# A two-layer decoder on one core: the third stage's queues written out in another order, with masks, maxima and row sums on eight heads at a time

## The chip, the cores and the metric

The kernel runs on one core of a Trainium2 chip. The metric is the device time of one execution in microseconds (us), and a kernel's figure is the median of several executions. A core has five engines that matter here, each with its own queue that it works off in order: TensorE (PE, with PEld for its weight loads), VectorE (DVE), ScalarE (ACT), GpSimd (POOL) and SyncE (SP), which here only issues DMAs. They meet through semaphores: an instruction can wait until a count is reached, and can raise one when it is done.

## The reference, cut to what matters

There are 16 sequences of 128 rows by 128 features (x), each with a context of 120 rows. Layer 0 is cross-attention and a feed-forward part; layer 1 is another cross-attention, with 16 heads of 64 and a relative position term, and a product in int8:

```python
hq, hk, hv = q @ Wq, k @ Wk, v @ Wv                      # q = layernorm(x); 16 heads of 64
attn = hq.hk + shift(hq.head_r) + hk.ub_w + shift(head_r.vb_w)
attn = where(mask, -INF, attn / sqrt(128)); attn = softmax(attn over the 120 context rows)
out = (attn @ hv) * sigmoid(q @ head_w)                  # a gate for each head
x = x + layernorm(out @ Wo + q) * ln_g + ln_b
x = x + dequantize(int8(layernorm(x)) @ int8(rhs))       # absmax scale of each row
```

All of it is float32 except the int8 product, whose integers travel as bfloat16.

## The kernel before

The work runs in three stages, one after another with some overlap: `attn0` (attention of layer 0), `ffn0` (its feed-forward part) and `layer1` (all of layer 1). In each the unit of work is one sequence t, 0 to 15, and the code is a software pipeline: `layer1(s, par)` is one step of the third stage, written out for every engine by hand, and each piece of it works on the sequence t = s - k for a lag k of its own. `run_steps` calls the steps s = -2 to 23; `on(t)` drops the pieces whose t is outside 0 to 15, so the first and last steps hold little. Steps 10 and 11 are the body of a loop of one round; it has no bearing on the order. What orders the work is thus only the order in which the pieces stand in each engine's `layer1`, and the waits.

A sequence passes through the stage so. DVE and POOL form the layer norm (`rstd`, `xn`), PE transposes it (`xnT`). PE forms queries (`hq_ps`, halves of 8 heads), keys (`hk_ps`) and values (`hv_ps`); ACT and DVE move them out of PSUM as `qv`, `qu`, `kT`, `hv`. PE multiplies `qv` by the position table `rT` (`rel_ps`, four groups of 32 products); ACT copies the results to `relw`; SP stores them to DRAM (`store`) and reads them back shifted (`shifted`, giving `relr`). PE forms the content scores (`content`), DVE adds `relr` to them (`added0` to `added3`, four heads of 120 columns each), applies the mask (`masked`), and takes the negative maxima (`nmax`). ACT exponentiates head by head with the row sum in `ssum`, in pairs of heads (`exp_heads`). DVE turns `ssum` and the gate's `ez` into a factor (`fden`, `rsum`), POOL scales the probabilities with it (`scale_probs`, four heads at a time, L381), PE transposes them (`probT_ps`), ACT copies them (`probT`), PE multiplies by `hv` (`av`), ACT copies (`oT_pairs`), PE applies `wo` (`y_ps`), DVE adds `xn_all` (`u`) and takes statistics (`ovar`). POOL and DVE finish the norm (`rstd_o`, `onorm`, `og`, `x_done`), and then come the norm and the quantization for the int8 part (`xf`, `tiny`, `qx`, `qxi`), its transpose and product (`qT_ps`, `acc_ps`), and the output (`fin`, stored by SP).

The tiles prob, nmax, ssum, rsum, ez, relw, relr, qv, qu, kT, hv are rings of two. PSUM is one tensor PS of eight banks, and `freed(...)` in front of a product waits until the bank's last reader is through; which bank a product writes and whom it waits for is part of the order.

Each of mask, maximum and row-sum factor works on one group of four heads in this kernel, so a step has four masks (DVE L995, L855, L878, L901), four maxima (L858, L861, L937, L945) and four pairs of factor and reciprocal (L843 to L850, L883 to L890).

## Time and profile before

| | us |
|---|---|
| runs of the kernel (three) | 459.0, 452.06, 458.26; median 458.26 |
| the profiled execution | 454.79 |
| its span, first to last instruction | 453.0 |
| PE busy | 415.2 (92% of the span) |
| DVE busy | 398.8 (88%) |
| ACT busy | 375.1 (83%) |
| POOL busy | 264.2 (58%) |

The third stage fills the span from about 165 us on. The profile is of one execution: 1.79 us of its time lie outside the span. Busy time of PE overstates it a little, since matmuls overlap and their ends are modelled; of a wait it is told which instruction ended it.

### The profile page before, as it was taken

Reading aid. Unit: us, or ns where it says so; the run is one execution under the profiler, and the core shown is the slowest. Engines: PE = TensorE matmul, PEld = TensorE weight load, DVE = VectorE, ACT = ScalarE, POOL = GpSimd, SP = SyncE. Lnnn points to the kernel's source line nnn. Section 1 sums busy time; section 2 is a strip of 40 time slices with the busy share of each in tenths; the row PEclk is TensorE's granted clock in tenths of the full one; section 3 lists DMA queues with packets and bytes.
Section 4 is the critical chain, followed back from the end, with each engine's and each line's share of the span. In section 5 each row is a group of like instructions: output and inputs, shape, how many; then the busy total and the mean of one; then the engine's idle time right before and its main releaser. Section 6 shows DMA issues by size and latency. Waiting matters only on the chain.

```text
span 453.0 us, 16761 instructions
## 1 busy us (share of the span) xinstructions
PE 415.2 (92%) x6147; PEld 313.1 (69%) x6147; DVE 398.8 (88%) x1300; ACT 375.1 (83%) x1483; POOL 264.2 (58%) x370
## 2 busy tenths in 40 slices
PE   7999999998789998889999999989999989998871
PEld 6555556555457777778888877868887878887560
DVE  5899999989679985799789999999999999999855
ACT  1999999998845556699989989988998999898941
POOL 4388888878966640044346357447447545646775
PEclk9999999999899999999999999999999999999796
DMA  7250000000000005887447564754754754764000
GB/s 213 58 193 26 14 11 6 11 8 15 2 2 0 0 2 138 216 208 205 120 106 191 156 146 120 190 133 104 198 134 110 198 147 94 186 163 100 8 7 23
DMA packets 54392, 44.88 MB, mean 99 GB/s; under 512 B 43952, under 2 KB 49328, under 8 KB 54320
## 3 DMA queue, kind: packets, MB, share of 16 engines
q1 hardware_dynamic: 53616, 43.59, 37.8%
q8 instruction: 46, 0.75, 0.7%
q10 hardware_dynamic: 704, 0.32, 0.3%
q14 instruction: 26, 0.21, 0.2%
HBM read 22.92 MB, written 20.97 MB: 97 GB/s over the span
## 4 chain that ended last, share of the span: by engine, by line
PE 44%; DVE 44%; issue 4%; ACT 3%; POOL 2%; DMA 1%; SPq 1%; POOLq 0%; DVEq 0%; ACTq 0%
PE PS L1003 37%; DVE prob L855 3%; PE PS L1019 3%; DVE xf L906 2%; DVE prob L901 2%; PE PS L1213 2%; DVE prob L989 1%; DVE nmax L861 1%; PE PS L1179 1%; DVE prob L995 1%; DVE prob L878 1%; DVE prob L865 1%; DVE prob L867 1%; DMA wr<-in_wr 1%; DVE qu L896 1%
## 5 line engine op out<-in xcount | busy, mean ns | idle before, releaser
L381 POOL TENSOR_TENSOR prob<-prob,rsum 128x480 f32<-128x480 f32 x64 | 69.1, 1091 | 85.4 <-DVE rsum L846 80.9
L533 ACT ACTIVATE prob<-prob,nmax 128x120 f32<-128x120 f32 x256 | 102.3, 440 | 1.0 <-DVE nmax L937 1.0
L449 ACT ACTIVATE prob<-PS,nmax 128x120 f32<-128x120 f32 x256 | 89.6, 394 | 4.3 <-DVE nmax L769 2.6
L324 POOL TENSOR_TENSOR prob<-prob,rsum 128x480 f32<-128x480 f32 x64 | 62.5, 988 | 23.2 <-DVE rsum L742 12.8
L533 ACT ACTIVATION_READ_ACCUMULATOR prob<-prob,nmax 128x1 f32 x256 | 63.0, 246 | 0.0
L449 ACT ACTIVATION_READ_ACCUMULATOR prob<-PS,nmax 128x1 f32 x256 | 61.5, 240 | 0.0
L1003 PE MATMUL PS<-rT,qv 64*32 64x152 f32 x2048 | 42.7, 293 | 5.8 <-DVE uo L933 3.8
L1003 PEld LDWEIGHTS PS<-rT,qv 64*32 64x32 f32 x2048 | 30.6, 105 | 21.6 <-issue 18.5
L1003 PEld LDWEIGHTS PS<-xnT,wq 128*128 128x128 f32 x288 | 37.1, 191 | 8.8 <-issue 7.3
L1003 PE MATMUL PS<-xnT,wq 128*128 128x128 f32 x288 | 42.7, 284 | 0.1
L1003 PE MATMUL PS<-ctx,wk 128*128 128x120 f32 x288 | 41.0, 278 | 0.0
L1003 PE MATMUL PS<-wv,ctx 128*120 128x512 f32 (+1 forms) x96 | 40.3, 501 | 0.0
L1003 PE MATMUL PS<-probT,hv 120*64 120x128 f32 x512 | 36.4, 286 | 3.2 <-ACT probT L618 3.2
L1003 PE MATMUL PS<-kT,qu 64*128 64x120 f32 x512 | 35.8, 279 | 3.0 <-ACT relw L632 2.0
L1003 PEld LDWEIGHTS PS<-ctx,wk 128*128 128x128 f32 x288 | 35.9, 191 | 2.2 <-issue 2.2
L1003 PE MATMUL PS<-wo,oT_pairs 128*128 128x128 f32 x256 | 35.9, 284 | 1.0 <-ACT oT_pairs L568 1.0
L1003 PE MATMUL PS<-relw,qT 32*128 32x480 f32 x128 | 34.4, 613 | 0.4 <-DVE relw L747 0.4
L1003 PEld LDWEIGHTS PS<-probT,hv 120*64 120x64 f32 x512 | 28.3, 140 | 8.8 <-ACT probT L618 3.7
L1003 PEld LDWEIGHTS PS<-kT,qu 64*128 64x128 f32 x512 | 31.5, 188 | 4.2 <-ACT relw L632 2.6
L1003 PEld LDWEIGHTS PS<-wo,oT_pairs 128*128 128x128 f32 x256 | 31.9, 196 | 2.5 <-ACT oT_pairs L568 1.8
L1019 PEld LDWEIGHTS PS<-ident,prob 64*120 64x120 f32 x512 | 18.2, 138 | 19.1 <-issue 19.1
L416 POOL TENSOR_TENSOR rstd<-ve,mhalf 128x1 f32<-128x1 f32 x16 | 8.7, 544 | 34.4 <-DVE ve L660 34.4
(195 smaller groups left out, 1128.5 us busy)
## 6 DMA issues: line engine op xcount, KB each, us to landing
rel_scratch<-relw SPq DMA_DIRECT2D x128, 152.0 KB, 3.1
relr<-rel_scratch SPq DMA_DIRECT2D x64, 240.0 KB, 4.2
ctx<-in_ctxT SPq DMA_DIRECT2D x32, 60.0 KB, 1.9
out_x<-fin SPq DMA_DIRECT2D x16, 64.0 KB, 3.2
x_all<-in_x SPq DMA_DIRECT2D x1, 640.0 KB, 7.1
wr<-in_wr SPq DMA_DIRECT2D x1, 512.0 KB, 5.4
wq<-in_wq SPq DMA_DIRECT2D x1, 512.0 KB, 3.6
wk<-in_wk SPq DMA_DIRECT2D x1, 512.0 KB, 4.4
```

The lines of the kernel that those rows point to most:

```text
L324: return pool.tensor_tensor(pr, pr, cols(rsum[p], g, HG).unsqueeze(2).to_broadcast([S, HG, SK]), ALU.mult)
L381: return pool.tensor_tensor(pr, pr, cols(rsum[p], g, HG).unsqueeze(2).to_broadcast([S, HG, SK]), ALU.mult)
L416: pool.tensor_tensor(rstd[p][:, 0:1], ve[p][:, 0:1], mhalf[:, :], ALU.pow).then_inc(A1["rstd"], 1)
L449: last = act.activation(cols(prob[p], n, SK), cols(scores, q, SK), ACT.Exp, bias=nmax[p][:, n:n + 1], accum_out=ssum[p][:, n:n + 1])
L533: last = act.activation(cols(pr, n, SK), cols(pr, n, SK), ACT.Exp, bias=bias[:, n:n + 1], accum_out=total[:, n:n + 1])
L855: dve.scalar_tensor_tensor(out=sc, in0=cap[p][:, :].unsqueeze(1).to_broadcast([S, HG, SK]), scalar=NEG, in1=sc, op0=ALU.add, op1=ALU.min). ...
L861: dve.tensor_reduce(out=cols(nmax[p], 1, HG), in_=heads(cols(prob[p], 1, HG * SK), HG), op=ALU.max, axis=AX.X, negate=True).then_inc(A1["n ...
L901: dve.scalar_tensor_tensor(out=sc, in0=cap[p][:, :].unsqueeze(1).to_broadcast([S, HG, SK]), scalar=NEG, in1=sc, op0=ALU.add, op1=ALU.min). ...
L906: dve.tensor_scalar(xf[p][:, :], row(x_all, t), mv3[p][:, 0:1], rstd3[p][:, :], ALU.subtract, ALU.mult)\
L1003: return pe.matmul(o, a, b, start=start, stop=stop)
L1019: last = pe.transpose(PS[0:SK, bank, q * S // 2:(q + 1) * S // 2], cols(prob[p], g * HG + q, SK)[rows], ident_sb[rows, rows])
L1213: last = pe.transpose(PS[0:SK, bank, q * S // 2:(q + 1) * S // 2], cols(prob[p], g * HG + q, SK)[rows], ident_sb[rows, rows])
```

## The change

Only `layer1` changes, in all five queues, and with it `run_steps`, which calls one step less.

1. The pieces stand in another order on every engine, and in other PSUM banks. Some work on another sequence within a step: the first half of the queries (`hq_ps`, `qv0`, `qu0`) on t = s + 1 in place of s; the last two groups of position products on s - 1 in place of s; one half of the values on s - 1 in place of s - 2; the quantization's first part (`xf` to `inv`) on s - 5 in place of s - 6, its product on s - 6 in place of s - 7. The exponentials of heads 8, 9, 12 and 13, before on s - 2, are now on s - 3 like those of 10, 11, 14 and 15, so all of the second half's stand in one step.
2. The four position groups have a semaphore each (`rel_ps0` to `rel_ps3`).
3. Mask, maximum and factor work on eight heads at a time: two of each in a step, 960 and 8 columns wide, in place of four. The four additions of `relr` stay as they are, four heads each. POOL still scales four heads at a time, but two of the four scalings now wait for nothing but the one before.

The core of the diff:

```diff
-            peeled(layer1, LOOPS[2][1], NB + 8)
+            peeled(layer1, LOOPS[2][1], NB + 7)
...
 @block.gpsimd, layer1:
-                    pool.wait_ge(A1["rsum"], 4 * t + 1)
+                    pool.wait_ge(A1["rsum"], 2 * t + 1)
+                    scale_probs(p, 0).then_inc(A1["scaled0"], 1)
                     scale_probs(p, 1).then_inc(A1["scaled1"], 1)
...
 @block.vector, layer1:
                     dve.wait_ge(A1["probs"], 4 * t + 2)
-                    dve.scalar_tensor_tensor(out=cols(rsum[p], 1, HG), in0=cols(ez[p], 1, HG), scalar=1.0,
-                                             in1=cols(ssum[p], 1, HG), op0=ALU.add, op1=ALU.mult).then_inc(A1["fden"], 1)
-                    dve.wait_ge(A1["fden"], 4 * t + 1)
-                    dve.reciprocal(cols(rsum[p], 1, HG), cols(rsum[p], 1, HG)).then_inc(A1["rsum"], 1)
...
+                    dve.scalar_tensor_tensor(out=cols(rsum[p], 0, 2 * HG), in0=cols(ez[p], 0, 2 * HG), scalar=1.0,
+                                             in1=cols(ssum[p], 0, 2 * HG), op0=ALU.add, op1=ALU.mult).then_inc(A1["fden"], 1)
+                    dve.wait_ge(A1["fden"], 2 * t + 1)
+                    dve.reciprocal(cols(rsum[p], 0, 2 * HG), cols(rsum[p], 0, 2 * HG)).then_inc(A1["rsum"], 1)
...
-                    dve.wait_ge(A1["added1"], t + 1)
-                    sc = heads(cols(prob[p], 1, HG * SK), HG)
+                    dve.wait_ge(A1["added0"], t + 1)
+                    sc = heads(cols(prob[p], 0, 2 * HG * SK), 2 * HG)
...
-                    dve.tensor_reduce(out=cols(nmax[p], 0, HG), in_=heads(cols(prob[p], 0, HG * SK), HG), op=ALU.max, axis=AX.X,
+                    dve.tensor_reduce(out=cols(nmax[p], 0, 2 * HG), in_=heads(cols(prob[p], 0, 2 * HG * SK), 2 * HG), op=ALU.max, axis=AX.X,
```

DVE, at a step of the full pipeline, before: from the mask of the first four heads to that of the last four. prob is the scores' tile, rsum the factor, cap the mask, nmax the maxima.

```order
L995 SCALAR_TENSOR_TENSOR prob<-cap,prob 128x480 [waits a1_added0]
L843 SCALAR_TENSOR_TENSOR rsum<-ez,ssum 128x4 [waits a1_probs]
L846 RECIPROCAL rsum<-rsum 128x4 [waits a1_fden]
L847 SCALAR_TENSOR_TENSOR rsum<-ez,ssum 128x4
L850 RECIPROCAL rsum<-rsum 128x4 [waits a1_fden]
L855 SCALAR_TENSOR_TENSOR prob<-cap,prob 128x480 [waits a1_added1]
L858 TENSOR_REDUCE nmax<-prob 128x4 [waits a1_masked]
L861 TENSOR_REDUCE nmax<-prob 128x4 [waits a1_masked]
L865 TENSOR_TENSOR prob<-PS,relr 128x480 [waits a1_relr11,a1_content]
L867 TENSOR_TENSOR prob<-PS,relr 128x480
L872 TENSOR_SCALAR uo<-uo,mv_o,rstd_o 128x128 [waits a1_orstd]
L878 SCALAR_TENSOR_TENSOR prob<-cap,prob 128x480 [waits a1_added3]
```

The same place now, where a step of DVE begins:

```order
L858 SCALAR_TENSOR_TENSOR rsum<-ez,ssum 128x8 [waits a1_probs]
L861 RECIPROCAL rsum<-rsum 128x8 [waits a1_fden]
L866 SCALAR_TENSOR_TENSOR prob<-cap,prob 128x960 [waits a1_added0]
L869 TENSOR_REDUCE nmax<-prob 128x8 [waits a1_masked]
L874 TENSOR_SCALAR uo<-uo,mv_o,rstd_o 128x128 [waits a1_orstd]
L879 TENSOR_SCALAR qx<-xf,tiny 128x128 [waits f1_inv]
L881 TENSOR_SCALAR xf<-qx 128x128 [waits f1_round]
L883 TENSOR_SCALAR qxi<-xf 128x128 [waits f1_clip]
L887 COPY kT<-PS 128x480 [waits a1_hk_ps]
```

The first half's factor is two instructions in place of four, mask and maximum are one each and 960 wide, and the finish of the norm (uo) and the quantization (qx, xf, qxi) stand right behind them. The second half's factor and mask now stand in the middle of the step, with the additions of the next sequence's first heads behind:

```order
L928 SCALAR_TENSOR_TENSOR rsum<-ez,ssum 128x8 [waits a1_probs]
L931 RECIPROCAL rsum<-rsum 128x8 [waits a1_fden]
L936 SCALAR_TENSOR_TENSOR prob<-cap,prob 128x960 [waits a1_added2]
L943 TENSOR_TENSOR prob<-PS,relr 128x480 [waits a1_probT_ps,a1_relr01,a1_content]
L948 TENSOR_TENSOR uo<-PS,xn_all 128x128 [waits a1_y_ps]
L952 TENSOR_REDUCE nmax<-prob 128x8 [waits a1_masked]
L956 TENSOR_TENSOR prob<-PS,relr 128x480
L961 BN_STATS stat_o<-uo 128x6 [waits a1_u]
L663 MEMSET gap 128x1 [waits a1_ostats]
L964 BN_AGGR mv_o<-stat_o 128x2
L966 TENSOR_SCALAR ve_o<-mv_o 128x1 [waits a1_ostats]
L972 TENSOR_SCALAR qu<-PS,ub 128x512 [waits a1_qv1]
```

Before, the four scores' additions stood in two pairs; now the pair for the first eight heads (L943, L956) has the output's addition (L948) and the maxima (L952) between, and the factor of the second half waits for all exponentials of its sequence.

POOL over a whole step, before:

```order
L381 TENSOR_TENSOR prob<-prob,rsum 128x480 [waits a1_rsum]
L390 TENSOR_TENSOR rstd_o<-ve_o,mhalf 128x1 [waits a1_ovar]
L394 TENSOR_TENSOR xb<-x_all,ln_b 128x128
L381 TENSOR_TENSOR prob<-prob,rsum 128x480 [waits a1_rsum]
L402 TENSOR_TENSOR uo<-uo,ln_g 128x128 [waits a1_onorm]
L404 TENSOR_TENSOR gap_pool<-mhalf 128x1 [waits a1_og]
L406 TENSOR_TENSOR x_all<-xb,uo 128x128
L381 TENSOR_TENSOR prob<-prob,rsum 128x480 [waits a1_rsum] x2
L416 TENSOR_TENSOR rstd<-ve,mhalf 128x1 [waits a1_var]
L420 TENSOR_TENSOR fin<-fin,rhs_scale 128x128 [waits f1_deq]
```

and now:

```order
L381 TENSOR_TENSOR prob<-prob,rsum 128x480 [waits a1_rsum]
L381 TENSOR_TENSOR prob<-prob,rsum 128x480
L391 TENSOR_TENSOR uo<-uo,ln_g 128x128 [waits a1_onorm]
L393 TENSOR_TENSOR gap_pool<-mhalf 128x1 [waits a1_og]
L395 TENSOR_TENSOR x_all<-xb,uo 128x128
L399 TENSOR_TENSOR fin<-fin,rhs_scale 128x128 [waits f1_deq]
L401 TENSOR_TENSOR gap_pool<-mhalf 128x1 [waits f1_deq2]
L403 TENSOR_TENSOR fin<-x_all,fin 128x128
L381 TENSOR_TENSOR prob<-prob,rsum 128x480 [waits a1_rsum]
L411 TENSOR_TENSOR rstd<-ve,mhalf 128x1 [waits a1_var]
L381 TENSOR_TENSOR prob<-prob,rsum 128x480
L418 TENSOR_TENSOR rstd_f<-ve_f,mhalf 128x1 [waits f1_var]
```

The scalings that stood apart (1, 1, 2) now stand 2, 1, 1, and the output's two products (L399, L403) come between the first pair and the third, right behind the norm's (L391, L395).

## Rows read from the trace of the kernel before

**Rows 1.** Windows: busy us (instructions) of PE, PEld, DVE, ACT, POOL; clock, DMA share, GB/s.

```profile
320.00:360.00 40.00, 38.88 (x674) 32.66 (x665) 38.78 (x110) 37.28 (x140) 22.30 (x33) 1.00 0.66 167
```

**Rows 2.** Timeline of DVE: mask L855, first in steps 2, 6, 14, 17 (start, duration).

```profile
185.17 0.65 DVE L855 SCALAR_TENSOR_TENSOR prob<-cap,prob 128x480 f32<-128x480 f32 x1
...
239.94 1.40 DVE L855 SCALAR_TENSOR_TENSOR prob<-cap,prob 128x480 f32<-128x480 f32 x1
...
371.66 1.40 DVE L855 SCALAR_TENSOR_TENSOR prob<-cap,prob 128x480 f32<-128x480 f32 x1
...
416.61 1.40 DVE L855 SCALAR_TENSOR_TENSOR prob<-cap,prob 128x480 f32<-128x480 f32 x1
```

**Rows 3.** Timeline of DVE, one full step.

```profile
321.12 0.65 DVE L995 SCALAR_TENSOR_TENSOR prob<-cap,prob 128x480 f32<-128x480 f32 x1
321.69 0.15 DVE L843 SCALAR_TENSOR_TENSOR rsum<-ez,ssum 128x4 f32<-128x4 f32 x1
...
322.24 1.40 DVE L855 SCALAR_TENSOR_TENSOR prob<-cap,prob 128x480 f32<-128x480 f32 x1
323.56 0.64 DVE L858 TENSOR_REDUCE nmax<-prob 128x4 f32<-128x480 f32 x1
...
326.63 0.44 DVE L883 SCALAR_TENSOR_TENSOR rsum<-ez,ssum 128x4 f32<-128x4 f32 x1
...
328.11 1.09 DVE L901 SCALAR_TENSOR_TENSOR prob<-cap,prob 128x480 f32<-128x480 f32 x1
329.12 1.00 DVE L906 TENSOR_SCALAR xf<-x_all,mv_f,rstd_f 128x128 f32<-128x128 f32 x1
330.16 0.29 DVE L909 TENSOR_REDUCE tiny<-xf 128x1 f32<-128x128 f32 x1
...
331.96 0.28 DVE L933 TENSOR_TENSOR uo<-PS,xn_all 128x128 f32<-128x128 f32 x1
332.16 0.64 DVE L937 TENSOR_REDUCE nmax<-prob 128x4 f32<-128x480 f32 x1
...
334.50 0.34 DVE L960 TENSOR_SCALAR xn<-x_all,mv,rstd 128x128 f32<-128x128 f32 x1
```

**Rows 4.** Timeline of POOL, same step: the scalings by rsum.

```profile
322.14 0.99 POOL L381 TENSOR_TENSOR prob<-prob,rsum 128x480 f32<-128x480 f32 x1 [4.94 <-DVE rsum L846]
...
327.70 2.35 POOL L381 TENSOR_TENSOR prob<-prob,rsum 128x480 f32<-128x480 f32 x2
```

**Rows 5.** Timeline of PE, one step at which the chain runs over PE.

```profile
374.50 1.09 PE L1003 MATMUL PS<-probT,hv 120*64 120x128 f32 x16
...
381.44 1.28 PE L1003 MATMUL PS<-rT,qv 64*32 64x152 f32 x64
...
384.21 1.12 PE L1003 MATMUL PS<-rT,qv 64*32 64x152 f32 x49
...
386.35 1.09 PE L1003 MATMUL PS<-probT,hv 120*64 120x128 f32 x16
...
390.93 1.09 PE L1003 MATMUL PS<-probT,hv 120*64 120x128 f32 x16
```

**Rows 6.** Timeline of ACT, two heads' exponentials.

```profile
323.76 0.42 ACT L533 ACTIVATE prob<-prob,nmax 128x120 f32<-128x120 f32 x1
...
324.14 0.41 ACT L533 ACTIVATE prob<-prob,nmax 128x120 f32<-128x120 f32 x1
```

**Rows 7.** Timeline of DVE, the stage's first addition.

```profile
183.46 0.66 DVE L989 TENSOR_TENSOR prob<-PS,relr 128x480 f32<-128x480 f32 x1 [2.49 <-DMA relr<-rel_scratch]
```

**Rows 8.** Timeline of DVE, the drain: first factor of step 18, last u.

```profile
427.42 0.15 DVE L843 SCALAR_TENSOR_TENSOR rsum<-ez,ssum 128x4 f32<-128x4 f32 x1
...
441.31 0.29 DVE L933 TENSOR_TENSOR uo<-PS,xn_all 128x128 f32<-128x128 f32 x1 [2.89 <-PE PS L1003]
```

**Rows 9.** Timeline of PE, the drain: a group of products with wo.

```profile
427.80 2.07 PE L1003 MATMUL PS<-wo,oT_pairs 128*128 128x128 f32 x8
```

**Rows 10.** Windows, the drain; columns as in Rows 1.

```profile
424.00:432.00 8.00, 7.05 (x58) 5.64 (x58) 5.79 (x28) 5.55 (x23) 6.00 (x13) 0.57 0.03 9
```

More of the change, by code:

```diff
@@ L275, in layer1 @@
                 if on(t):
+                    sp.wait_ge(A1["relw1"], t + 1)
+                    store(t, p, 0)
                     after(sp, A1["hv_ps"], 2 * t - 2)
@@ new lines, in layer1 @@
+                t, p = s - 2, par
+                if on(t):
+                    dve.wait_ge(A1["added2"], t + 1)
+                    sc = heads(cols(prob[p], 1, 2 * HG * SK), 2 * HG)
+                    dve.scalar_tensor_tensor(out=sc, in0=cap[p][:, :].unsqueeze(1).to_broadcast([S, 2 * HG, SK]), scalar=NEG, in1=sc,
+                                             op0=ALU.add, op1=ALU.min).then_inc(A1["masked"], 1)
+                t, p = s - 1, 1 - par
+                if on(t):
+                    dve.wait_ge(A1["content"], 2 * t + 1)
+                    dve.wait_ge(A1[f"relr0{p}"], 2 * loads(t, p))
+                    after(dve, A1["probT_ps"], 2 * t - 3)
+                    dve.tensor_tensor(cols(prob[p], 1, HG * SK), PS[:, 5, 0:HG * SK], cols(relr[p], 1, HG * SK), ALU.add)\
+                       .then_inc(A1["added1"], 1)
@@ new lines, in layer1 @@
+                t, p = s - 4, par
+                if on(t):
+                    dve.wait_ge(A1["y_ps"], t + 1)
+                    dve.tensor_tensor(uo[p][:, :], PS[:, 7, 0:D], row(xn_all, t), ALU.add).then_inc(A1["u"], 1)
+                t, p = s - 2, par
+                if on(t):
+                    dve.wait_ge(A1["masked"], 2 * t + 2)
+                    dve.tensor_reduce(out=cols(nmax[p], 1, 2 * HG), in_=heads(cols(prob[p], 1, 2 * HG * SK), 2 * HG), op=ALU.max, axis=AX.X,
+                                      negate=True).then_inc(A1["nmax"], 1)
@@ L985, in layer1 @@
[L985 to L996 removed]
+                    dve.wait_ge(A1["qv0"], t + 1)
@@ L997, in _ @@
+                    dve.tensor_scalar(cols(qu[p], 0, 512), PS[:, 1, :], ub_sb[:, :], SCALE1, ALU.add, ALU.mult)\
+                       .then_inc(A1["qu0"], 1)
             run_steps(dve, attn0, ffn0, layer1, crossing)
@@ new lines, in layer1 @@
+                t, p = s, par
+                if on(t):
+                    pe.wait_ge(r_set, 4)
+                    pe.wait_ge(A1["qu0"], t + 1)
+                    freed(pe, (A1["oT0"], t - 3, t - 4), (A1["qu1"], t, t - 1))
+                    if at_step(t, 0):
+                        pe.wait_ge(F0["hidT"], NB - 1)
+                    for m in (2, 3):
+                        for e, bank in ((0, 4), (1, 1)):
+                            half_ = slice(e * DK, (e + 1) * DK)
+                            for a in range(S // BLK):
+                                u0 = S - BLK * (a + 1)
+                                last = mm(PS[a * BLK:(a + 1) * BLK, bank, (m % 2) * WIN:(m % 2 + 1) * WIN],
+                                          qv[p][half_, m * S + a * BLK:m * S + (a + 1) * BLK], rT[half_, m, u0:u0 + WIN])
+                    last.then_inc(A1["rel_ps1"], 1)
@@ new lines, in layer1 @@
+                t, p = s - 1, 1 - par
+                if on(t):
+                    pe.wait_ge(A1["kT0"], t + 1)
+                    freed(pe, (A1["probT2"], t - 2, t - 3), (A1["relw2"], t + 1, t))
+                    for m in range(0, 4):
+                        for e, bank in ((0, 2), (1, 5)):
+                            half_ = slice(e * DK, (e + 1) * DK)
+                            last = mm(PS[:, bank, (m % 4) * SK:(m % 4 + 1) * SK], cols(qu[p], m, S)[half_], cols(kT[p], m, SK)[half_])
+                    last.then_inc(A1["content"], 1)
```

721 lines of the change are left out of this document (334 added, 387 removed), and 11 rows, old and new, of the table A1.

## The prediction

> **What bounds the kernel now.** I read the table of windows first, then the starts of one instruction in each step, then one step of each engine. In the full pipeline nearly everything is busy: of 40 us PE has 38.88, DVE 38.78, ACT 37.28, POOL 22.30 [rows 1]. So the question is not which engine is busiest but which one never waits. The mask L855 stands once in each step. From step 6 to step 14 it starts at 239.94 and 371.66: eight steps of 16.47 us [rows 2]. In those steps DVE shows no idle time, and the chain of waits runs over DVE alone. Steps 2 to 5 take 54.77 us together, steps 14 to 16 take 44.94 [rows 2]; in the latter the chain runs partly over PE. What goes before step 2 and behind step 17 (some 19 and 36 us of the stage) is fill and drain.
>
> DVE's step is not all work. Back to back, an instruction of 480 columns costs 0.57 us: L995 starts at 321.12 and the next at 321.69. But L855, the same instruction, holds DVE for 1.32 (322.24 to 323.56), L901 for 1.01 and the small L906 for 1.04, where a like one, L960, is through in 0.34; L883 takes 0.44 where L843 takes 0.15 [rows 3]. What they share is POOL: a scaling starts at 322.14, a pair at 327.70 [rows 4]. DVE waits until POOL's instruction is through. The losses are 0.75 + 0.44 + 0.68 + 0.29 = 2.16 us a step, so DVE's own work is 16.47 - 2.16 = 14.31.
>
> PE is close behind. Between two `av` products (374.50 and 390.93) lie 16.43 us in which the 64 position products at 384.21 took 2.14 until the next row, against 1.28 for those at 381.44 [rows 5]. Without that wait of 0.86 a PE step is 15.57. ACT's busy share gives 37.28/40 x 16.47 = 15.35 [rows 1], of which some is overlap of neighbours.
>
> **The change, part by part.** *Wider masks and maxima.* L933 with 128 columns is followed after 0.20 us, an instruction of 480 after 0.57 [rows 3]: 352 columns are 0.37, so 480 are 0.50 and the fixed part is 0.07. Two masks and two maxima fewer: 4 x 0.07 = 0.26 saved. The durations of 0.65 would say 0.15 each, 0.6 in all, but they overlap the next instruction; the distance of the starts decides. The Trainium skill (VectorE: DVE Perf Modes, the section on the TRN2 errata) says that the fixed cost is exposed between instructions and measured at about 150 cycles of a 0.96 GHz clock; that would be 4 x 0.157 = 0.63 us. The rows speak against it here. Against the saving, the maximum now follows its own mask at once and waits for its end, which its duration of 0.65 against the 0.57 puts at 0.1. The copy xn_all no longer follows xn directly, which gives 0.1 back.
>
> *Factors.* From L843 to L855 four small instructions take 0.55 [rows 3]; one STT and one reciprocal take half of it and a little more, 0.29. Twice a step: 0.52 saved. DVE's own work becomes 14.31 - 0.26 - 0.52 = 13.53.
>
> *What waits for POOL.* In the new order a scaling still becomes free in the same moment as a mask, twice a step: I price each at L855's 0.75. The first pair of scalings runs as one behind the other; in [rows 3, 4] DVE gets in between two such scalings (L901 in the middle of the 2.35 us pair), so I take one loss, not two. The second collision is new in place: L936 behind L931. L883 and L906 lose theirs (0.96 saved): the second scaling falls under the maximum, which reads one operand and shows no wait beside POOL, and `xf` comes when POOL has long had its short instructions. In return `onorm` frees POOL's four 128-column products while `qx`, `xf`, `qxi` and `xn` run on DVE, all of the kind of L906. Bounds: 0.2 (one wait for the rest of a short product) to 0.9 (each waits for one of 0.45). I take 0.5. Sum: 1.5 + 0.5 = 2.0 in place of 2.16, and a DVE step of **15.5 to 15.6** (bounds 15.2 and 16.0).
>
> *PE's order.* The products are the same, 15.57 a step. The four position groups now stand together at the start of the step, in eight different banks, so PE no longer waits for ACT's `relw` copies between them (the 0.86 above); in return `content` of the second half waits for `relw1`, the transposes for `relw2`. Laying the new queues end to end with exponentials at 0.38 a head [rows 6] and the PE rows above, ACT ends the `relw` copies 3.6 us into its step and PE asks for them at 3.9 to 4.4, DVE asks for the second content at 6.1 and PE has it at 5.4, DVE wants all exponentials at 8.1 and ACT has them at about 8.2, PE wants bank 7 (`u`) at 12.1 and DVE frees it at 11.1. All fits within some tenths, on the condition that PE leads DVE by 0.3 to 0.9 us. With two engines at 15.5 and such small reserves I take **15.7** a step, between the floor of 15.57 and the 16.47 of now. Eight steps: 8 x 0.77 = **6.1 us**, bounds 0 and 7.2.
>
> *Steps 2 to 5* (54.77): PE's work in them is about 10.5, 11.5, 15.4 and 15.5, of which the first two will have waits; I take 1.0 saved, bounds -0.5 and 1.5. *Steps 14 to 16* (44.94): PE still full in 14, then without the next sequence's queries, 15.6 + 14.8 + 13.3 = 43.7, so 1.2 saved, bounds 0 and 2.
>
> *Fill.* The first addition waits 2.49 us for relr, until 183.46 [rows 7]: the SP queue stores the second half of relw before it reads the first half back. Now the read of the first half is issued before that store, and the two last groups come a step later anyway. But `qv0` and `qu0` of sequence 0 now stand in step -1, ahead of `ffn0`'s last pieces on PE, ACT and DVE, which costs about 1.5 us on ACT's `hidT` copy, and PE then starts the position products where it started them before. I take 0.7 saved, bounds -1.5 and 2.
>
> *Drain.* Step 18 begins at 427.42, and the last `u` is at 441.31 [rows 8], 13.9 us. About 1.8 of it is clock: eight products with wo take 2.07 [rows 9] in a stretch of 8 us with a mean granted clock of 0.57 [rows 10], that is the lower level (1.2 GHz) for most of it; at the upper one they would be half, and the `av` products behind them too, 2 x 0.9. Ahead of it PE's busy share had fallen. In the new order ACT's queue sets the pace there (eight exponentials, six copies) and the last `u` comes 10.5 us behind the step's start. What follows `u` is the same chain in both, and it is the chain and not the number of steps that counts: the step less is worth nothing of itself. If the clock falls again I save 1.6, if not 3.4; I take **2.5**, bounds 0 and 4.
>
> **Sum:** 6.1 + 1.0 + 1.2 + 0.7 + 2.5 = 11.5 us. Against the profiled execution that is 454.8 - 11.5 = 443.3. The four times shown spread from 452.06 to 459.0, mean 456.0, median of three 458.26, so the profiled one is a fast one; I set the sum against the mean: **444.5 us**, 2.5% less.
>
> **The rivals.** *The gain is eaten by waits between PE, ACT and DVE.* For it speaks that all three have over 92% [rows 1] and that DVE now holds its whole queue twice on the last exponentials (`rsum` on eight heads, where four would have let the rest go on); against it the reserves above. Steps then stay at 16.1 to 16.4, worth 0.6 to 3, and with the ends 3 to 6 in all: about 451.5.
>
> *The factor's wait turns the ring over, slower.* L928 waits for the exponentials of all of heads 8 to 15. ACT has them at 8.2 in its step and DVE asks at 8.1. ACT in turn waits for PE at nearly each copy. If these waits add up to more than about 1 us a step, ACT's queue of 14.6 us work comes to over 15.6, and DVE waits with everything behind: maxima, `qu`, and so PE's next position products. From about 1.9 us on it eats all that the change gives; at 2.4 us the step is 17.0, eleven steps at +0.5 cost 5.5 and the ends give 2 back: 459.5.
>
> *POOL keeps DVE out for a whole pair of scalings.* The two first scalings now have no wait between them. If DVE lost both, 0.95 more at one place a step, the step would be 16.5, as now, and the time some 452. The Trainium skill (SBUF — State Buffer, the section "SBUF: two separate sides") says that the shared ports are locked for one whole instruction and the loser blocks fully, which would allow either; the 1.09 of L901 between two scalings [rows 3] speaks for one.
>
> *Nothing is done as said* I exclude: the queues show two masks of 960 in a step in place of four.
>
> **How the numbers follow.** Forecast (savings of 7 to 17) 0.62; waits eat it (451.5) 0.22; POOL pair (452) 0.06; ring turned over (459.5) 0.10. Range: the forecast's bounds, 7.4 + 1.5 + 2 + 1 + 4 = 16 at best and the spread of the executions give 438; upward it takes in the two middle rivals, 455. A measurement here tells about 2% from no change, 9.1 us. Of the forecast nine tenths lie beyond that, and little of the rest: faster 0.60, within 2% 0.31, slower 0.09.
>
> **What would show it.** Masks of 960 columns start 15.7 us apart from step 6 on, alternately 1.9 long (1.1 of work and 0.75 of wait), and the maxima 1.1 without wait; `qx` or `xf` beside POOL longer than 0.3; the first factor and the mask behind it with no idle ahead; PE with less than 0.3 us of idle a step; the first addition at about 181; last `u` 10 to 12 us behind the start of step 18. It would be wrong if DVE shows idle time ahead of L928 or L905, if the mask takes 2.8, or if the step stays above 16.2.

## The result, and the profile after

The changed kernel takes **452.08 us** (median of 20 runs, 448.96 to 457.44) against 457.34 for the kernel before (20 runs beside it, 452.06 to 459.45): a ratio of 0.990, 95% interval 0.987 to 0.993. The forecast was 444.5 against some 456, 2.5% less; 1.0% came. The profiled execution took 455.68 us with a span of 453.9, longer than the one of before (453.0), so the two traces are not the place to look for the 1%. They are the place to look for where things went.

The page: busy time by engine (us, share of the span, instructions), the one instruction queue with 46 packets of 16 KB (that it carries PE's program is shown below), the chain of what ended last.

```profile
PE 417.1 (92%) x6147; PEld 317.7 (70%) x6147; DVE 371.9 (82%) x1172; ACT 377.0 (83%) x1483; POOL 271.3 (60%) x370
...
q8 instruction: 46, 0.75, 0.7%
...
PE 75%; DVE 11%; ACT 5%; issue 3%; POOL 2%; DMA 1%; SPq 1%; POOLq 0%
```

DVE fell from 88% to 82%, and the chain is now PE's. The same 40 us as in [rows 1] (windows, same columns):

```profile
320.00:360.00 40.00, 39.70 (x743) 33.30 (x741) 35.86 (x97) 38.26 (x138) 24.87 (x36) 1.00 0.66 145
```

PE went from 38.88 to 39.70 of 40, DVE from 38.78 to 35.86. Timeline of DVE, the first mask of steps 2, 6, 14 and 17, as in [rows 2]:

```profile
188.38 1.15 DVE L866 SCALAR_TENSOR_TENSOR prob<-cap,prob 128x960 f32<-128x960 f32 x1
...
245.42 1.11 DVE L866 SCALAR_TENSOR_TENSOR prob<-cap,prob 128x960 f32<-128x960 f32 x1
...
373.13 1.11 DVE L866 SCALAR_TENSOR_TENSOR prob<-cap,prob 128x960 f32<-128x960 f32 x1
...
419.71 1.11 DVE L866 SCALAR_TENSOR_TENSOR prob<-cap,prob 128x960 f32<-128x960 f32 x1
```

With these starts and those of [rows 2] the span falls into five pieces. The three last columns belong to experiments below (`after_reads_first2`, `after_less_dma`, `factors_only`); each column is one profiled execution.

| us | before | forecast | after | reads of relr ahead of ctx, but for both ends | most of the relr data left out | old order, factors alone |
|---|---|---|---|---|---|---|
| start of step 2 | 185.17 | -0.7 | 188.38 | 188.53 | 188.89 | 185.90 |
| steps 2 to 5 | 54.77 | -1.0 | 57.04 | 57.01 | 54.89 | 54.10 |
| steps 6 to 13 | 131.72 | -6.1 | 127.71 | 124.01 | 124.13 | 125.77 |
| steps 14 to 16 | 44.94 | -1.2 | 46.58 | 44.40 | 43.21 | 43.70 |
| step 17 to the end | 36.35 | -2.5 | 34.16 | 34.17 | 34.16 | 34.82 |
| span | 453.0 | | 453.9 | 448.1 | 445.3 | 444.3 |

The steps that nothing disturbs are 15.50 long (310.49 to 326.00), shorter than the 15.7 of the forecast. But the mean of steps 6 to 13 is 15.96, and steps 4, 7, 8 and 15 take 18.5, 17.0, 17.0 and 17.9. What lengthens them stands in PE's timeline (start, duration, idle time ahead and what ended it):

```profile
260.06 1.09 PE L1000 MATMUL PS<-probT,hv 120*64 120x128 f32 x16
261.09 2.31 PE L1000 MATMUL PS<-rT,qv 64*32 64x152 f32 x128
263.33 1.15 PE L1000 MATMUL PS<-ctx,wk 128*128 128x120 f32 x8
264.41 0.69 PE L1210 MATMUL PS<-ident,prob 64*120 64x64 f32 x16
264.94 0.88 PE L1000 MATMUL PS<-kT,qu 64*128 64x120 f32 x11
267.04 0.49 PE L1000 MATMUL PS<-kT,qu 64*128 64x120 f32 x5 [1.23 <-issue]
...
280.33 0.82 PE L1000 MATMUL PS<-ctx,wk 128*128 128x120 f32 x5
282.51 0.48 PE L1000 MATMUL PS<-ctx,wk 128*128 128x120 f32 x3 [1.36 <-issue]
...
215.12 0.45 PE L1000 MATMUL PS<-rT,qv 64*32 64x152 f32 x3 [1.85 <-issue]
...
395.65 0.94 PE L1000 MATMUL PS<-wo,oT_pairs 128*128 128x128 f32 x7 [1.63 <-issue]
```

PE stops in the middle of a group, where it waits for nothing that the profile shows ("issue"): 11 content products, 1.23 us of nothing, and the other 5. From 165 us on, PE's idle stretches put down to issue add up to 8.6 us, against 3.5 before. Five of them, at 215.12, 267.04, 282.51, 345.57 (0.30) and 395.65, make 6.4 us and are the subject here. The other three (0.82 at 178.36, 0.83 at 204.42, 0.53 at 424.81) are as long in the kernel with little data below, and what makes them is not shown. Behind two of the five, PE's granted clock falls to its lower level (1.2 GHz) for 3.4 us, at 216.2 and 397.1, so that the clock column of the windows reads 0.66 and 0.58:

```profile
216.00:221.00 5.00, 5.00 (x50) 4.50 (x51) 2.63 (x9) 4.67 (x21) 0.00 (x0) 0.66 0.56 144
398.00:401.00 3.00, 3.00 (x36) 2.93 (x35) 0.11 (x1) 1.55 (x6) 2.68 (x4) 0.58 0.48 136
```

Each such fall, 3.4 us at half the clock, adds 1.7 us to an engine that never waits. Over the 20 runs time and mean granted clock go together (r = -0.95).

Now DVE beside POOL, one step (DVE's timeline, then POOL's), as in [rows 3, 4]:

```profile
310.18 0.16 DVE L858 SCALAR_TENSOR_TENSOR rsum<-ez,ssum 128x8 f32<-128x8 f32 x1
310.37 0.20 DVE L861 RECIPROCAL rsum<-rsum 128x8 f32<-128x8 f32 x1
310.49 1.11 DVE L866 SCALAR_TENSOR_TENSOR prob<-cap,prob 128x960 f32<-128x960 f32 x1
311.63 1.15 DVE L869 TENSOR_REDUCE nmax<-prob 128x8 f32<-128x960 f32 x1
312.70 0.77 DVE L874 TENSOR_SCALAR uo<-uo,mv_o,rstd_o 128x128 f32<-128x128 f32 x1
...
318.38 0.17 DVE L928 SCALAR_TENSOR_TENSOR rsum<-ez,ssum 128x8 f32<-128x8 f32 x1 [0.57 <-ACT prob L531]
...
318.71 1.11 DVE L936 SCALAR_TENSOR_TENSOR prob<-cap,prob 128x960 f32<-128x960 f32 x1
```

```profile
310.66 2.73 POOL L381 TENSOR_TENSOR prob<-prob,rsum 128x480 f32<-128x480 f32 x2 [2.35 <-DVE rsum L861]
...
318.87 1.79 POOL L381 TENSOR_TENSOR prob<-prob,rsum 128x480 f32<-128x480 f32 x1 [3.09 <-DVE rsum L931]
...
321.14 0.98 POOL L381 TENSOR_TENSOR prob<-prob,rsum 128x480 f32<-128x480 f32 x1
```

The forecast had the mask wait 0.75 us for the scaling, twice a step. Here the mask starts 0.17 us ahead of the scaling and takes 1.11, its own length; POOL waits in its place (1.79 and 2.73 where 0.98 and twice that would do), and POOL has time.

### The profile page after: what moved, and what is told of

Its sections match the earlier page's. It is cut to its first block, busy times and chain, and to the rows that moved or that the text cites. A ratio compares the mean times of both kernels' runs of the same rounds, so it can differ in the third digit from the quotient of the medians.

```text
span 453.9 us, 16613 instructions
## 1 busy us (share of the span) xinstructions
PE 417.1 (92%) x6147; PEld 317.7 (70%) x6147; DVE 371.9 (82%) x1172; ACT 377.0 (83%) x1483; POOL 271.3 (60%) x370
## 4 chain that ended last, share of the span: by engine, by line
PE 75%; DVE 11%; ACT 5%; issue 3%; POOL 2%; DMA 1%; SPq 1%; POOLq 0%
PE PS L1000 66%; PE PS L1210 3%; PE PS L1016 3%; ACT prob L531 2%; PE PS L1176 1%; DMA wr<-in_wr 1%; DVE relr L767 1%; DVE nmax L719 1%; DVE nmax L721 1%; POOL prob L324 1%; DVE relw L762 1%; PE PS L1346 1%; PE PS L1166 1%; DVE nmax L690 1%; PE PS L1126 1%
## 5 line engine op out<-in xcount | busy, mean ns | idle before, releaser
L381 POOL TENSOR_TENSOR prob<-prob,rsum 128x480 f32<-128x480 f32 x64 | 86.3, 1360 | 88.8 <-DVE rsum L931 52.0
L531 ACT ACTIVATE prob<-prob,nmax 128x120 f32<-128x120 f32 x256 | 98.8, 403 | 0.0
L324 POOL TENSOR_TENSOR prob<-prob,rsum 128x480 f32<-128x480 f32 x64 | 62.4, 986 | 24.7 <-DVE rsum L757 12.7
L531 ACT ACTIVATION_READ_ACCUMULATOR prob<-prob,nmax 128x1 f32 x256 | 53.4, 208 | 0.0
L1000 PE MATMUL PS<-ctx,wk 128*128 128x120 f32 x288 | 42.2, 283 | 1.4 <-issue 1.4
L1000 PE MATMUL PS<-rT,qv 64*32 64x152 f32 x2048 | 38.1, 291 | 3.0 <-issue 2.7
L1000 PE MATMUL PS<-kT,qu 64*128 64x120 f32 x512 | 38.2, 290 | 2.6 <-issue 1.2
L1000 PE MATMUL PS<-wv,ctx 128*120 128x512 f32 (+1 forms) x96 | 39.1, 491 | 0.4 <-DVE uo L948 0.4
L1000 PEld LDWEIGHTS PS<-rT,qv 64*32 64x32 f32 x2048 | 32.1, 105 | 7.9 <-issue 7.8
L1000 PEld LDWEIGHTS PS<-kT,qu 64*128 64x128 f32 x512 | 33.0, 196 | 5.8 <-issue 3.8
L1016 PEld LDWEIGHTS PS<-ident,prob 64*120 64x120 f32 x512 | 18.5, 140 | 18.6 <-issue 18.6
L1016 PE MATMUL PS<-ident,prob 64*120 64x64 f32 x512 | 22.8, 231 | 4.9 <-POOL prob L324 3.5
```

What stands on the lines that cost most here:

```text
L324: return pool.tensor_tensor(pr, pr, cols(rsum[p], g, HG).unsqueeze(2).to_broadcast([S, HG, SK]), ALU.mult)
L381: return pool.tensor_tensor(pr, pr, cols(rsum[p], g, HG).unsqueeze(2).to_broadcast([S, HG, SK]), ALU.mult)
L531: last = act.activation(cols(pr, n, SK), cols(pr, n, SK), ACT.Exp, bias=bias[:, n:n + 1], accum_out=total[:, n:n + 1])
L1000: return pe.matmul(o, a, b, start=start, stop=stop)
L1016: last = pe.transpose(PS[0:SK, bank, q * S // 2:(q + 1) * S // 2], cols(prob[p], g * HG + q, SK)[rows], ident_sb[rows, rows])
```

## The experiments

Medians are set against the kernel before, run beside each group of them (medians 457.01, 456.74, 456.93 and 458.67 us).

**The change in its two halves.** The order and the width can be had apart. `merge_only` is the old order with masks, maxima and factors on eight heads; `order_only` is the new order with pieces of four:

```diff
 # merge_only, DVE, old order
-  stt(cols(rsum[p], 1, HG) ...); reciprocal; stt(cols(rsum[p], 0, HG) ...); reciprocal
+  stt(cols(rsum[p], 0, 2 * HG) ...); reciprocal
-  mask(g) and nmax(g) on cols(prob[p], g, HG * SK), g = 0..3
+  mask(h) and nmax(h) on cols(prob[p], h, 2 * HG * SK), h = 0, 1
```

> The queues of the kernel before, in their old order, with mask, maximum and row-sum factor on eight heads at a time: the second half of the change alone. Theory A (the gain comes from taking DVE off the bound, and then PE is the bound, which in the changed kernel loses what it gets to stretches in which it waits for its own instructions): DVE's step loses 0.8 us of work, the step falls from 16.47 to about 15.9, ratio to before 0.985 to 0.995, and PE shows idle put down to issue. Rival B (the order makes the gain, the merge is worth nothing since it adds waits for all exponentials and both additions): ratio 0.997 to 1.01, DVE idle ahead of the factor or the masks.

> The changed kernel's queues with mask, maximum and factor taken back to four heads at a time, at the same places. Theory A: DVE's step in the new order has more than 1 us of reserve against PE's 15.5, of which the four-head pieces use 0.8, so the time is that of the changed kernel within 0.5% (ratio to before 0.985 to 0.995), with the same stretches of 1 to 2 us in which PE waits for its instructions. Rival B (the eight-head pieces are what made the step 15.5): step 16.0 to 16.4, ratio 0.998 or above.

Measured: `merge_only` 446.49 us (6 runs), ratio 0.978 (0.974 to 0.983); `order_only` 454.60 (12 runs), ratio 0.996 (0.992 to 1.000). Both lie outside the ranges of their first theories, the width on the better side and the order on the worse. The width alone, in the order that was there, gives more than twice what the whole change gives. In it the wide masks of the first half take 1.10 as well, and the step is 15.74. In the new order without the width the step is 15.95: DVE's two masks in a row lose the port between them, the second takes 1.44 (profile of `order_only`, DVE):

```profile
315.88 0.63 DVE L950 SCALAR_TENSOR_TENSOR prob<-cap,prob 128x480 f32<-128x480 f32 x1
316.43 1.44 DVE L953 SCALAR_TENSOR_TENSOR prob<-cap,prob 128x480 f32<-128x480 f32 x1
```

So the new order can only use its shorter step with the wide pieces, but something in it costs what they bring.

**The transfers.** The gaps of the changed kernel lie where its DMA engines are full. The round trip of the position scores through DRAM was cut to a few columns, in the new order and in the old (from the third sequence on these kernels leave out most of the relative term, and their output is wrong):

```diff
-  out_to = ... [[ROW, BLK], [1, R // 2]]
+  out_to = ... [[ROW, BLK], [1, w]]          # w = 8 from sequence 2 on
-  src = ... [[ROW - 1, S // 2], [WIN, H // 2], [1, SK]]
+  src = ... [[ROW - 1, S // 2], [WIN, n], [1, w]]    # n = 1, w = 8 from sequence 2 on
```

> The changed kernel, in which from the third sequence on the relative term's round trip moves 8 columns of each row in place of all (the term is then wrong for those sequences; every wait stays). Theory C (PE's idle put down to issue, 6 us in the stage, is its instruction loads, delayed by the queue's stores and reads that fill the DMA engines): the gaps of 1.2 to 1.9 us go, no fall of the granted clock follows them, time 5 to 9 us below the changed kernel's 452.1, ratio to before 0.97 to 0.98. Rival D (the loads are late because the 128 position products and their weight loads, 256 instructions in 2.3 us, run faster than instructions can be loaded, whatever the DMA engines do): the gaps stay at half their length or more, time within 3 us of 452.1.

> The same cut of the round trip in the kernel before. Theory C with DVE as the bound: PE's short gaps go, but DVE sets the step of 16.47, so the time stays within 3 us of before, ratio 0.993 to 1.0; the reads that DVE waits for at the start of the stage are those of the first two sequences and stay. Rival (transfers slow ACT or DVE themselves): steps below 16.2, ratio under 0.985.

> Leaves out most of the data of the round trip of relw to relr from the third sequence on (8 columns per transfer in place of 304 and 960), in the kernel that has the old order and the wider pieces. Theory A (the transfers cost time only where they delay PE's instruction loads, and that takes the new order, in which both halves are read back in one go): almost nothing to gain here, 444 to 446 us against 446.5 with the full transfers, and the stage step stays at 15.7, because it is set by the position products that follow ACT. Rival B (the transfers slow any kernel that is bound by PE): a gain like the one in the new order, 7 us, so 439 to 441.

Measured: new order 444.80 us (5 runs), ratio 0.973 (0.967 to 0.978); before 458.17 (10 runs), ratio 1.001 (0.998 to 1.005); `merge_only` 447.0 (4 runs, 444.65 to 452.13), ratio 0.985 (0.978 to 0.993), against 446.5 with all data. The data cost the new order 7.3 us and the old order nothing that stands clear of the noise, with wide pieces or without. In the new order with little data, steps 6 to 13 take 124.13, and of the five gaps four are gone. The first stays, 1.24 us in place of 1.85, and with it theory C is not the whole: there the DMA engines are all but idle, and the packet, the 16th, ends at 213.45 (profile of `after_less_dma`: PE, and a window with the columns of [rows 1]).

```profile
211.51 2.28 PE L1003 MATMUL PS<-rT,qv 64*32 64x152 f32 x125
215.03 0.45 PE L1003 MATMUL PS<-rT,qv 64*32 64x152 f32 x3 [1.24 <-issue]
```

```profile
211.50:215.00 3.50, 2.29 (x127) 1.98 (x125) 2.78 (x5) 2.54 (x8) 2.73 (x2) 1.00 0.05 6
```

So PE can run out of instructions by its own pace, where a border falls at the end of its 128 position products, and no fall of the clock followed this shorter gap. The data lengthen that gap and make the others. Windows of the DMA queues from 263.8 to 265.4 us, each around one packet of the instruction queue, of the changed kernel and then of the same with little data (queue, packets, MB, share of the 16 engines):

```profile
q1 hardware_dynamic: 581, 0.27, 99.7%
q8 instruction: 1, 0.02, 5.3%
```

```profile
q1 hardware_dynamic: 144, 0.00, 4.9%
q8 instruction: 1, 0.02, 4.2%
```

That packet of 16 KB, the 23rd of 46, runs from 264.15 to 265.50 us in the changed kernel, and PE goes on at 267.04. Ahead of the other four gaps a packet ends 1.5 to 1.8 us before PE goes on, too. In the trace with little data, which runs the same PE program, the 21st packet begins when PE has started 3352 entries of its queue other than products (weight loads, mostly), with all data 3396; for the 23rd it is 3599 and 3660, for the 25th 3861 and 3929. PE came from the one count to the other in 1.1 to 2.6 us, so the packets start that much late behind the data. In `after_reads_first2` below, which has all the data but reads `relr` earlier, the 21st and the 23rd start at 3357 and 3599 again, and the 25th at 3830.

That these packets are what PE waits for shows in the places of the gaps, counted in all entries of PE's queue from the start (products, weight loads, and waits and other entries of its sequencer): 7042, 7554, 9859 and 11650 in `order_only` (263.45, 278.92, 342.51 and 392.62 us), 8578, 10882 and 11394 before, 9090 and 10370 in two kernels of the old order. Within an order all distances are multiples of 256, to within one: 512, 2305, 1791; 2304, 512. And the packets agree: in the changed kernel the gap at entry 5250 follows the 16th packet, that at 7042 the 23rd, at 7554 the 25th and at 11650 the 41st, which is 256 entries for each packet. A packet of 16 KB holds 256 instructions, and each of these gaps stands at such a border. The longer stretches of issue elsewhere (0.83 at 204.42 in the changed kernel, 1.04 at 412.53 before) do not, and are something else.

**The reads' place.** SP issues the reads of both halves of `relr` behind one another, and behind the load of the next context, which waits for `hv_ps` (SP's issues in the changed kernel):

```profile
258.25 0.35 SPq L232 DMA_DIRECT2D ctx<-in_ctxT  x1
...
259.12 2.61 SPq L261 DMA_DIRECT2D relr<-rel_scratch  x4
```

Two microseconds later PE begins its 128 position products (261.09), 256 instructions in 2.31 us, and wants the next packet at once. Three kernels of the new order move the reads: apart, one a step later, or ahead of the context.

```diff
 # after_reads_apart
+  sp.wait_ge(A1[f"relr1{1 - p}"], 2 * loads(t - 1, 1 - p))   # the other half has landed
   shifted(t, p, 0)
 # after_read0_later: in the next step, as in the old order
   store(t, p, 1)
+  sp.wait_ge(A1["stored0"], 64 * t + 64); shifted(t, p, 0)
 # after_reads_first
   store(t, p, 0)
-  after(sp, A1["hv_ps"], 2 * t - 2); load_context(t, p)
   shifted(t - 1, 1 - p, 1); shifted(t, p, 0)
+  after(sp, A1["hv_ps"], 2 * t - 2); load_context(t, p)
```

> The changed kernel, but SP issues the read of the first half of relr only when the read of the second half has landed; the same bytes, in two bursts of 2 us in place of one of 4. Theory A (an instruction load of PE waits behind the whole queue of data packets that stands before it, and the two reads in a row make it longest): the gaps of 1.2 to 1.9 us go or shrink to under 0.5, and the time falls by 3 to 7 us, to 445 to 449. Rival B (the sum of the traffic counts, not how it is bundled): 451 to 453, as the changed kernel. Third: the read now lands later, DVE's additions wait for it and the step grows: over 453.

> The changed kernel with SP's queue in the old order as to the reads: the first half of relr is read a step later, behind the store of the second half, so the two reads stand some 6 us apart and each has a store beside it. Theory A (bundling of the reads): 445 to 449 and few gaps. Rival B (sum of traffic): 451 to 453. Third: the read lands only about 1 us ahead of the addition that uses it, and the start of the stage loses the 0.7 us that the earlier read gave, so a late read could show as idle time of DVE ahead of the additions and 453 to 458.

> The changed kernel, but SP loads the next context and mask behind the two reads of relr and not ahead of them. That load waits for hv_ps, and the reads stand behind it: in the changed kernel they are issued at 259.1 to 261.7 and 276.1 to 278.7, just ahead of PE's 128 position products (261.1, 278.1), though the DMA engines had stood still since 270. Now they should be issued some 4 us earlier and land before those products begin. Theory A (PE's instruction loads come late behind the reads): the gaps at block ends go, the step is 15.5 from step 6 on, 445 to 448. Rival B (the sum of the traffic counts): 451 to 453. Third: the later context makes PE wait for its wk products: idle time ahead of them, 453 to 456.

Measured: apart 450.86 us (12 runs), ratio 0.988 (0.985 to 0.991); later 464.20 (6 runs), ratio 1.021 (1.016 to 1.026); first 452.15 (6 runs), ratio 0.990 (0.985 to 0.995). None of the three medians is in the range that theory A gave, and the first and the last lie at or in that of rival B; their traces tell more. *Apart* has three gaps at borders in place of five (1.33 at 217.44, 0.28 at 280.61, 0.98 at 344.11; 2.6 us in place of 6.4), but DVE waits 2.47 us for the first reads. *Later* fell to the third expectation and beyond its range: DVE waits in each step (profile of `after_read0_later`, DVE), and the step is 16.41:

```profile
294.66 0.66 DVE L941 TENSOR_TENSOR prob<-PS,relr 128x480 f32<-128x480 f32 x1 [0.98 <-DMA relr<-rel_scratch]
```

*First* has steps of 15.50, 15.51, 15.51 and no gap over 0.3 us from 211 to 404 us, but pays once at the start, where the context comes late and the clock falls behind the wait, at 205.4 for 3.4 us (profile of `after_reads_first`, PE):

```profile
205.20 1.02 PE L1000 MATMUL PS<-ctx,wk 128*128 128x120 f32 x4 [4.58 <-DMA ctx<-in_ctxT]
```

The next kernel puts the context ahead of the reads for the first four and the last two sequences only.

> The reads of relr ahead of the load of the next context in SP's queue, as in the last such kernel, which had no gap at a block end from step 5 on and steps of 15.50, but lost 4.6 us to one late context at 205 and 0.6 at 404 and a clock dip behind the former. Now that load keeps its old place for the first four and the last two sequences and goes behind the reads only between. Theory A (the gaps come from PE's instruction loads behind the reads, and nothing else in the middle of the stage costs time): the 4.6 and 0.6 are back, the gap of about 1.8 at 215 may return, the middle stays at 15.50 a step: 446 to 449, level with the 445.8 of the old order with wider factors. Rival B (the new order costs something beyond this, or the gaps return elsewhere): 450 to 452. Nothing is left out of the computation.

Measured: 449.59 us (6 runs), ratio 0.981 (0.977 to 0.986), the best of the new order with all its work and nearly twice the gain of the change as made (9.1 us against 5.3, each against the kernel before beside it; the two medians themselves lie 2.5 apart). Its trace holds its own control. In the middle SP issues the reads at 270.22, long before PE's position products; at both ends the old order of SP stands. The gaps are at the ends and nowhere between (profile of `after_reads_first2`: SP, PE, and the windows of [rows 1]):

```profile
270.22 3.52 SPq L261 DMA_DIRECT2D relr<-rel_scratch  x4
273.79 0.62 SPq L232 DMA_DIRECT2D ctx<-in_ctxT  x1
```

```profile
215.25 0.45 PE L1004 MATMUL PS<-rT,qv 64*32 64x152 f32 x3 [1.82 <-issue]
...
391.47 0.94 PE L1004 MATMUL PS<-wo,oT_pairs 128*128 128x128 f32 x7 [1.03 <-issue]
```

```profile
320.00:360.00 40.00, 40.00 (x767) 33.91 (x765) 36.51 (x102) 38.83 (x139) 24.48 (x38) 1.00 0.65 144
```

PE is busy 40.00 of 40 us beside a DMA share of 0.65, as much traffic as before: it is not the sum of the traffic but its place that makes the gaps in the middle.

**PE's instructions less dense.** The four position groups apart, two and two:

```diff
   rel_ps0, rel_ps2
+  hk_ps (wk products), probT_ps (transposes)
   rel_ps1, rel_ps3
-  hk_ps (wk products), probT_ps (transposes)
```

> The changed kernel, but PE's four position groups are no longer in one piece: two, then the wk products and the transposes, then the other two. The same instructions, waits and bytes. Theory A': every gap falls behind a block of 256 PE instructions most of which are position products (128 products with their weight loads, 2.31 us), and the next block of 16 KB is not there after so short a time; spread over 3.5 us or more the block lasts long enough. Then the gaps shrink to under 0.5, steps are 15.5 to 15.6 and the time 446 to 449. Rival B (how dense the instructions stand doesn't matter, the load comes late by itself): same gaps, 451 to 453. Third: PE now waits for ACT's relw copies before the second pair and the content products: idle time ahead of those, step 15.9 or more, 452 to 456.

Measured: 467.89 us (6 runs), ratio 1.025 (1.020 to 1.030). No gap is left at a block border (the 1.97 us put down to issue stand elsewhere, at 178.82, 207.31, 422.32 and 439.23), but this proves little, since PE now waits in each step for the ACT copies that have to come first, and the step is 17.24; the time lies beyond the 452 to 456 of the third expectation (profile of `after_spread`, PE):

```profile
285.32 1.12 PE L1000 MATMUL PS<-ctx,wk 128*128 128x120 f32 x8 [0.76 <-ACT relw L552]
...
288.64 1.16 PE L1000 MATMUL PS<-kT,qu 64*128 64x120 f32 x16 [0.37 <-ACT relw L564]
```

**Which of the wide pieces.** The old order, with the factors alone on eight heads, and with masks and maxima alone (the two halves of the diff of `merge_only`).

> The kernel before, with nothing changed but the factors (row sum times denominator, reciprocal): one pair of instructions on eight heads in place of two pairs on four, twice a step. By the sum of the prediction that is 0.52 us of DVE a step, over some 15 steps 5 to 8 us where DVE is the bound: 450 to 452. If the waits for POOL just shift with it, or if PE takes over at once (its products that follow ACT make 15.7 a step), less: 453 to 456. The masks and maxima alone would then bring the rest up to the 446.5 of both.

> The kernel before, with nothing changed but the masks and the maxima: one of 960 columns in place of two of 480, twice a step; the factors stay on four heads. The factors alone gave 445.8, as much as both together (446.5). By the sum of the prediction the masks and maxima save 0.26 less 0.1 of DVE's own work: a step of 16.3 and 453 to 455. Rival: any small relief of DVE brings the step down to the 15.7 that PE allows in the old order, because a wait for POOL goes with it: 446 to 448. Third: DVE gains nothing and the maxima of heads 0 to 3 come later for ACT: 457 to 460.

Measured: factors 445.83 us (4 runs), ratio 0.978 (0.973 to 0.983), the fastest of all kernels that do the whole work, level with `merge_only`; masks and maxima 454.75 (10 runs), ratio 0.998 (0.994 to 1.002), nothing. The sum of the prediction had put the factors alone at 450 to 452, for it priced their work and no wait. Here DVE, then POOL, of `factors_only`:

```profile
318.60 0.61 DVE L851 SCALAR_TENSOR_TENSOR prob<-cap,prob 128x480 f32<-128x480 f32 x1
```

```profile
318.76 1.29 POOL L381 TENSOR_TENSOR prob<-prob,rsum 128x480 f32<-128x480 f32 x1 [4.97 <-DVE rsum L846]
```

and of `masks_only`:

```profile
321.35 1.90 DVE L855 SCALAR_TENSOR_TENSOR prob<-cap,prob 128x960 f32<-128x960 f32 x1
```

```profile
321.25 0.99 POOL L381 TENSOR_TENSOR prob<-prob,rsum 128x480 f32<-128x480 f32 x1 [4.31 <-DVE rsum L846]
```

With factors on four heads the first reciprocal frees POOL while DVE still has the second pair to do: POOL starts at 321.25, the mask comes 0.10 us later and waits 0.8; the step is 16.53. With factors on eight heads the one reciprocal stands right ahead of the mask, and the mask is first by 0.16. The wide factor saves 0.5 us of instructions and, by that, also the 0.75 of a wait at the first mask.

## Why the prediction was wrong, by its own steps

**What fails first: PE's order.** "The products are the same, 15.57 a step. The four position groups now stand together": the floor was right (15.50 measured), and so was the end of the waits for `relw`. The step from there to 15.7 counted waits between PE, ACT and DVE, and PE's own instruction stream in none of its terms. The 128 products in one piece use up 256 instructions in 2.31 us, and the reads of `relr`, which the change had put together and just ahead of them, hold the next 16 KB up. The prediction put this at nothing, without a reason. By the table that cost steps 6 to 13 3.7 us (127.71 against 124.01 with the reads moved), so the term was 4.0 in place of 6.1; with the reads moved it is 7.7. In *steps 14 to 16* it cost 2.2 to 3.4 (the 1.63 at 395.65 and the clock behind it): a loss of 1.6 for a gain of 1.2. In *steps 2 to 5* it cost 2.1 (57.04 against 54.89 with little data; the longer gap at 215 and the clock behind it): a loss of 2.3 for a gain of 1.0. The three make 8.0 to 9.2 in the profiled execution, where the clock fell twice behind such gaps. The 1.24 us of the gap at 215 that stay with little data come on top; without them *steps 2 to 5* would have given the 1.0 of the forecast. By the medians it is 452.1 - 444.8 = 7.3 (`after_less_dma`), of the 7.6 that are missing to the forecast (452.1 - 444.5). That the two nearly meet is partly luck: in that kernel's profile steps 6 to 13 give 7.6 where 6.1 was forecast, and the fill is 4.4 worse than forecast.

**DVE's sum: right in its own work, wrong in the waits, and without effect.** The factors take 0.31 (L858 to L866) for 0.29 forecast. The masks' starts to the next are 1.14 and 1.02, the maxima's 1.07 and 1.06, against 1.14 for two of the old ones: 0.27 saved, for 0.26 less 0.1. By the Trainium skill (VectorE: DVE Perf Modes, the section on the TRN2 errata) it would have been an estimated 0.63; the starts speak against it, as they did in [rows 3]. But "a scaling still becomes free in the same moment as a mask ... I price each at L855's 0.75" has the wrong one waiting: the mask comes first. The Trainium skill (SBUF — State Buffer, "SBUF: two separate sides") says that whichever of the two starts first has the shared port for its whole instruction; the trace agrees: 1.11 and 1.79 here, 1.90 and 0.99 with the mask 0.10 us behind. The 0.5 for small instructions beside POOL's came to 0.6, partly at another place: L874 takes 0.77 beside the second scaling, where a like one (L894) takes 0.34, and L881 0.39 in place of 0.23. DVE ended with more than 1 us a step to spare (35.86 busy of 40; 0.57 idle ahead of L928), and since PE is the bound, none of it counts. Idle time ahead of L928 or L905 was one of the forecast's own signs of being wrong, and it came: up to 0.66 ahead of L928 in nearly every step, 1.3 ahead of L905 in two.

**The fill** was to gain 0.7 and lost 3.2, 2.7 of it ahead of the first `xn` (168.48 against 165.74). Of these 1.4 are this execution's: its clock also fell at 11 us, that of `order_only` did not, and there the first `xn` stands at 167.12. Most of the rest, 1.2, goes with the work put ahead of `ffn0`'s last pieces: `factors_only`, in the old order and with its clock falling in the same place and for as long as in `order_only`, has it at 165.94; two others, neither with a fall ahead of it, differ by 0.8 (`masks_only` 164.13, `after_read0_later` 164.94). The forecast had 1.5 for this and set the earlier reads against it in full. They do bring the first addition forward, to 16.6 us behind the first `xn` from 17.7, but not the mask, which comes 19.9 behind it in place of 19.4.

**The drain** was to gain 2.5 and gained 2.2, for a reason only half foreseen. In `merge_only`, the old order with a clock that stays up until 435 us, the same piece takes 34.6, and in `masks_only`, where it stays up until 440, 35.0; the new order's 34.16 is thus worth 0.4 to 0.9, and the other 1.3 to 1.8 go with the clock that [rows 10] show. The forecast took the fall for 1.8 and the last `u` for 10.5 us behind the start of step 18; it came 12.1 behind (430.08 to 442.14).

**The rivals.** "The gain is eaten by waits" had the time right (451.5) and the place wrong: DVE does not wait for ACT in a way that counts. So the number was met by another mechanism than the rival's. The ring did not turn over: L928 waits 0.57. POOL does not keep DVE out. The best case of the range adds up 7.4 and 1 where the terms' own bounds are 7.2 (the steps) and 2 (the fill); it would be 16.7 in place of 16, which changes nothing.

**What the change could have been.** One part of it, the wide factors, carries the gain: 445.8. The new order has the shorter step (15.50 against 15.72 for `factors_only`), which is 1.8 us in steps 6 to 13, and gives it back with its later start (2.6) and, even with the reads moved, in steps 2 to 5 (2.9, the gap at 215 and the clock behind it in them).

## What stays open

When PE asks for a packet of instructions is not in the trace. That the density of its instructions matters, and not only the data ahead of the packet, shows by itself in one gap alone, the 1.24 us at 215.03 with little data; for the others it rests on their places (all five of the changed kernel in the 128 position products or at most 41 products behind) and on the old order, which has as much data and few gaps. Shifting the block borders by half a block was not tried. Nor was the new order with its first steps put right.

## What to carry to other kernels

When a change brings the busiest engine near 100%, ask for its instruction stream too: how many instructions it takes in a microsecond at its densest, and which transfers run just then. A gap that the profile puts down to "issue", in the middle of a group of like products, is the sign; count all entries of the queue, waits included, between two such gaps. And where two engines share a port, look at which of them is released first: an instruction moved by 0.1 us ahead of the other's release turned a wait of 0.75 on the bound into one on an engine with time to spare. A change in several parts is best measured in its parts: here the smallest gave more than the whole.

## What the runs showed of the hardware that was not expected

- PE's program comes in 16 KB packets of 256 instructions, 0.9 to 1.7 us each on the DMA engines in the changed kernel's third stage, and PE goes on 1.5 to 1.8 us after a late one has ended. Beside full data queues the 21st, 23rd and 25th packet start 1.1 to 2.6 us later in PE's own progress than beside nearly empty ones. Behind 125 of 128 position products PE waits 1.24 us for one even at a DMA share of 0.05.
- A gap of 1.6 to 1.9 us in a PE that is otherwise full was followed by 3.4 us at the lower clock in the changed kernel (215.12, 395.65), and so was the 1.82 at 215.25 with the reads moved; those of 1.23 and 1.36 were not. It is not a rule: PE waited 2.09 us at 200.48 in `after_reads_apart` and 1.81 at 419.03 in `merge_only`, and the clock stayed up.
- Starts 0.10 to 0.17 us apart decide which of DVE and POOL waits, and for one instruction: mask 1.11 and scaling 1.79, or scaling 0.99 and mask 1.90.
